# A gated attention and mixture-of-experts layer: the experts' scatter adds its rows to the residual rows already stored in the output

## The chip, the cores and the metric

The kernel runs on one core of one Trainium2 chip. The metric is the device time of one execution in microseconds (us); lower is better. The kernel before takes 298.14 us, the median of 3 runs (295.5 to 301.95).

## The reference, cut to what matters

There are 32 batches of 128 tokens with 128 features, so T = 4096 tokens, and 8 experts with room for 512 tokens each. A token that comes too late for its expert's room keeps its residual row unchanged.

```python
x = x + tanh(g_xattn[0]) * xattn(layernorm(x), ctx, ctx)    # 16 heads of 8, length 128
x = x + tanh(g_ffn[0])   * moe(layernorm(x))

def moe(tokens):                       # E = 8 experts, C = T / E = 512 places each
    gates = softmax(tokens @ Wg); idx = argmax(gates)
    loc = cumsum(one_hot(idx)) - 1     # the token's place with its expert; kept if loc < C
    hidden = relu(expert_in @ W1 + b1) # 128 -> 512
    expert_out = hidden @ W2 + b2      # 512 -> 128
    return gate * expert_out[idx, loc] # 0 for tokens that were not kept
```

## The kernel before, in words

The program is written by hand for each engine; semaphores are waited for in the order in which the code stands. It has two stages.

**Attention.** A loop over steps c from -8 to 39 runs a software pipeline over the 32 batches, in groups of four (GB = 4, eight groups). At step c the scores of batch c are computed on TensorE (PE, tile S, L482), and VectorE (DVE) takes their row maxima (L833, negm). One step later the maxima are transposed, split by ScalarE (ACT, L720) and DVE (L839) into two bf16 rows (tile mrow, 16 x 2 x 128), and SyncE (SP) sends them with two DMAs of 4 KB (L358) into the free rows of qp, the packed queries. After they have landed, PE computes the shifted scores of that batch (tile TS, L497, two steps after the batch began), ACT their exponentials (prob, L703), and PE the values (O, L513). For each group SP also packs the queries and keys of a coming group with 12 DMAs of 128 KB (L347, pack), loads x and the context (L377 and L372), and stores the finished residual rows x1 of an old group to the output (L368). All of these are on SP's one DMA queue.

Each group of tokens ends in a tile rec (three buffers, used in turn). A row of rec holds, in order, the normalised row (128 numbers), the residual row x1 (128) and 8 logits; the first logit's place is later overwritten by the gate, the second's by a code of the token's number. The first REC = 258 numbers of it are the token's record. GpSimd (POOL) scatters the records into rec_dram in device memory with indirect DMAs of 128 rows (scatter, L1224), at the place that the routing has found: expert times 512 plus place with that expert. Places that no token takes must read as zero, so POOL clears all of rec_dram beforehand with eight DMAs from a tile of zeros (zero_records, L1272), one in each of the steps c = 1 to 8. The scatter of the first group waits for them.

**Experts.** When all records have landed, SP loads for each expert e the normalised rows (load_xe, tile xe, 512 B a row) and, with a second DMA, the rest (load_xr, tile xr: residual row, gate, code; 520 B a row). PE transposes xe (turn, L608), computes the hidden layer (hidden, L618) and the outputs (outputs, L634); the order on PE is turn(e), outputs(e-2), hidden(e), so that the outputs of an expert come two turns after its rows (experts 5 and 6 then follow one another). DVE does half of the ReLUs (relus, L1110) and closes each expert: residual2(e) reads gate and code from xr, takes tanh(g_ffn) into the gate, turns the code into a token number (tok), and starts fin as b2 times gate plus the residual row (L1125, 4 instructions); finish(e, h) adds gate times the expert's output to half h of fin (L1140). POOL writes fin to the output with four indirect DMAs for each expert (rows_out, L1313), 128 rows of 512 B each. The tile fin has two buffers, so residual2(e) first waits until the four scatters of expert e-2 have landed (semaphore fin_out). The order on DVE is relus(e), finish(e-1, 0), residual2(e), finish(e-1, 1), and PE may write half h of the output banks again (X) after finish of the expert before (v_fin). After the last scatter SP waits for all of them and the program ends.

Of the kernel before, what the change touches and what calls it, by code (L numbers as in the profile page):

```python
# [32 lines left out]
REC = 2 * P + 2  # L33
# [3 lines left out]
def flamingo_kernel(nc, x, ctx_in, g_xattn, g_ffn, w_qkv, b_qkv, w_out, b_out, wg, w1, b1, w2, b2, consts, out):  # L37
# [4 lines left out]
    DE = D + E  # L42
    HEADS = 16
# [15 lines left out]
    with ExitStack() as ctx:  # L59
# [102 lines left out]
        xe = [sb(f"xe{i}", [P, ET, D]) for i in range(2)]  # L162
        xr = [sb(f"xr{i}", [P, ET, REC - D]) for i in range(2)]
# [3 lines left out]
        gate2 = [sb(f"gate2_{i}", [P, ET]) for i in range(2)]  # L167
        tok = [sb(f"tok{i}", [P, ET], U32) for i in range(2)]
# [34 lines left out]
        w1_in, w2_in, xe_in, xr_in, fin_out = sem2("w1_in"), sem2("w2_in"), sem2("xe_in"), sem2("xr_in"), sem2("fin_out")  # L203
# [90 lines left out]
        def _(sp):  # L294
# [54 lines left out]
            def step(c):  # L349
# [15 lines left out]
                if stores:  # L365
                    sp.wait_ge(v_x1, GB * (g - 2) + GB)
                    sl = bass.ds((g - 2) * GB, GB)
                    sp.dma_start(out_v[:, sl, :], rec[(g - 2) % 3][:, :, D:2 * D]).then_inc(x1_out[(g - 2) % 3], 16)  # L368
# [31 lines left out]
            for e in range(2):  # L400
                load_xr(e)
            sp.wait_ge(p_eT, 1)
            load_xe(2)

            for e in range(2, E):
                sp.wait_ge(p_H, 4 * (e - 1))
                load_w1(e)
                if e < E - 1:
                    sp.wait_ge(p_eT, e)
                    load_xe(e + 1)  # L410
                sp.wait_ge(p_Y, 2 * (e - 1))
                load_w2(e)
                sp.wait_ge(v_res, e - 1)
                load_xr(e)
# [7 lines left out]
        def _(pe):  # L422
# [179 lines left out]
            def turn(e):  # L602
# [4 lines left out]
                for t in range(ET):  # L607
                    mm = nc.tensor.transpose(S[:, e % 2, t * P:(t + 1) * P], xe[e % 2][:, t, 0:D], ident)  # L608
# [50 lines left out]
        def _(act):  # L659
# [45 lines left out]
            def step(c):  # L705
# [65 lines left out]
                if j == 1 and is_group(g - 2) and g - 2 < NG - 1:  # L771
# [3 lines left out]
                    nc.scalar.activation(rec[G % 3][:, :, 2 * D + 1], token_code[:, G * GB:(G + 1) * GB], ACT.Copy)  # L775
# [5 lines left out]
            def normed2(ks):  # L781
                for k in ks:
                    nc.scalar.activation(rec[(NG - 1) % 3][:, k, 0:D], rec[(NG - 1) % 3][:, k, D:2 * D], ACT.Identity,
# [6 lines left out]
            nc.scalar.activation(rec[(NG - 1) % 3][:, :, 2 * D + 1], token_code[:, (NG - 1) * GB:], ACT.Copy).then_inc(a_code, 1)  # L790
# [28 lines left out]
        def _(dve):  # L819
# [38 lines left out]
            def residual(n):  # L858
                dve.wait_ge(p_at, n + 1)
                dve.wait_ge(g_xb, n // GB + 1)  # L860
                G, row1 = n // GB, rec[n // GB % 3][:, n % GB, D:D + DE]
# [45 lines left out]
            def route(G):  # L907
# [4 lines left out]
                lgs = rec[G % 3][:, :, 2 * D:2 * D + E]  # L912
# [438 lines left out]
```

## Time and profile before

| What | us |
|---|---|
| median of 3 runs | 298.14 |
| the profiled execution, its own time | 298.6 |
| its span, first to last instruction | 296.5 |
| outside the span | 2.1 |
| attention, until the last residual row | about 207 |
| last routing, last records, first expert's rows | about 207 to 221 |
| experts on PE | 221 to 286.9 |
| last scatter's issue and landing, end | 286.8 to 296.5 |

Times in the profile are counted from the first instruction. PE is the matmul engine, PEld its weight loads, "SPq" and "POOLq" the time in which SyncE or GpSimd issue a DMA or wait in their instruction queue. PEclk is the clock that the chip granted to TensorE, as a share of 2.4 GHz. In the chain of waits each row is one piece of the chain that ended last; a row that begins with DMA is a transfer that something waited for.

### The profile page before, as it was taken

What the parts mean: (1) busy time and instruction counts of PE and PEld (TensorE: products, weight loads), DVE (VectorE), ACT (ScalarE), POOL (GpSimd) and SP (SyncE); (2) the same over time, 40 slices, a digit from 0 to 9 for tenths busy, and PEclk for the clock granted to TensorE, in tenths of its full rate; (3) what the DMA queues carried; (4) which work ended last, traced back from release to release, by engine and by line L of the source; (5) the groups of instructions that cost most, each with busy time, mean ns of one, the idle gap of its engine ahead of it and who ended that gap; (6) DMA issues with size and microseconds to landing.
All of it is one profiled execution on the core that took longest, in us unless ns stands there. A gap on an engine that the chain in (4) does not pass through costs nothing.

```text
span 296.5 us, 8184 instructions
## 1 busy us (share of the span) xinstructions
PE 244.5 (82%) x2907; PEld 163.5 (55%) x2907; DVE 196.6 (66%) x663; ACT 155.6 (52%) x375; POOL 182.3 (61%) x246
## 2 busy tenths in 40 slices
PE   1748758788979989999899989995869999999950
PEld 1325525465755755765656666663324677777740
DVE  4676717647978999989897999965302545555440
ACT  5553727567778787787887756681202322222100
POOL 6625916911982998897897968448720056555781
PEclk9998959969999999999999999999595999999995
DMA  4652771990482652661733541138352256554310
GB/s 120 184 162 73 214 217 32 237 293 19 113 235 57 174 158 71 195 182 46 213 110 90 152 126 57 58 102 174 138 144 66 71 170 188 173 180 132 103 55 16
DMA packets 50920, 39.27 MB, mean 132 GB/s; under 512 B 9698, under 2 KB 47223, under 8 KB 50880
## 3 DMA queue, kind: packets, MB, share of 16 engines
q1 hardware_dynamic: 47168, 28.67, 35.9%
q0 software_dynamic: 3712, 10.07, 10.4%
q8 instruction: 24, 0.39, 0.6%
q14 instruction: 16, 0.13, 0.2%
HBM read 13.72 MB, written 12.65 MB: 89 GB/s over the span
## 4 chain that ended last, share of the span: by engine, by line
PE 39%; DVE 13%; DMA 13%; SPq 10%; issue 9%; ACT 8%; POOL 4%; POOLq 0%; ACTq 0%; DVEq 0%
PE X L634 9%; DMA qp<-mrow 8%; DVE negm L833 6%; SPq L347 6%; PE TS L618 5%; PE M L546 3%; ACT prob L703 3%; PE O L513 3%; PE TS L497 3%; PE O L618 3%; PE M L618 2%; PE S L482 2%; PE X L441 2%; SPq L358 2%; POOL rec_dram L1224 2%
## 5 line engine op out<-in xcount | busy, mean ns | idle before, releaser
L703 ACT ACTIVATE prob<-TS 128x512 f32<-128x512 f32 x128 | 72.0, 589 | 40.1 <-PE TS L497 39.2
L833 DVE TENSOR_REDUCE negm<-S 128x4 f32<-128x512 f32 x128 | 81.6, 679 | 8.5 <-PE S L482 7.9
L513 PE MATMUL O<-prob,vals 128*32 128x128 f32 x1024 | 42.1, 283 | 0.8 <-ACT oraw L712 0.8
L1313 POOL DMA_INDIRECT out_dram<-fin,tok x32 | 31.5, 986 | 14.2 <-issue 12.2
L1224 POOL DMA_INDIRECT rec_dram<-rec,slot x32 | 32.2, 1005 | 8.0 <-issue 5.5
L497 PE MATMUL TS<-qp,kp 64*128 64x128 bf16 x512 | 28.1, 221 | 9.7 <-DMA qp<-mrow 9.6
L482 PE MATMUL S<-kp,qp 62*128 62x128 bf16 x512 | 31.3, 222 | 2.3 <-DVE negm L833 2.0
L513 PEld LDWEIGHTS O<-prob,vals 128*32 128x32 f32 x1024 | 24.6, 110 | 13.9 <-ACT prob L703 7.0
L267 POOL TENSOR_TENSOR rest_k<-full_k,parts_k 128x512 f32<-128x512 f32 x7 | 8.0, 1149 | 39.3 <-ACT parts_k L674 39.3
L804 ACT ACTIVATE qp<-TS,b_act 128x512 f32<-128x512 f32 x16 | 11.0, 687 | 39.9 <-PE TS L618 39.9
L634 PE MATMUL X<-w2s,qp 128*128 128x128 f32 x240 | 28.2, 275 | 0.9 <-issue 0.9
L634 PEld LDWEIGHTS X<-w2s,qp 128*128 128x128 f32 x240 | 27.4, 192 | 1.7 <-ACT qp L804 1.7
L482 PEld LDWEIGHTS S<-kp,qp 62*128 62x128 bf16 x512 | 18.0, 95 | 14.4 <-issue 6.3
L497 PEld LDWEIGHTS TS<-qp,kp 64*128 64x128 bf16 x512 | 19.1, 96 | 11.8 <-DMA qp<-mrow 11.3
L1168 POOL TENSOR_TENSOR fence_p<-pool_c 128x1 f32<-128x1 f32 x16 | 3.2, 201 | 27.6 <-DVE tok L1122 20.3
L618 PE MATMUL TS<-xeT,w1s 128*128 128x512 f32 x32 | 18.4, 659 | 1.4 <-ACT xeT L799 1.4
L1175 POOL TENSOR_TENSOR rs<-rs,pool_c 128x4 f32<-128x4 f32 x16 | 16.5, 1029 | 1.3
L1140 DVE SCALAR_TENSOR_TENSOR fin<-X,gate,fin 128x128 f32<-128x128 f32 x30 | 9.2, 345 | 11.8 <-PE X L634 11.8
L839 DVE TENSOR_TENSOR mrow<-M,mrow 16x128 bf16<-16x128 f32 x32 | 8.8, 275 | 11.9 <-ACT mrow L720 11.5
L546 PE MATMUL M<-cst,oraw 128*128 128x128 f32 x64 | 14.2, 304 | 2.3 <-DVE mrow L839 1.9
L683 ACT ACTIVATE xn<-x_sb,nm,rs 128x128 f32<-128x128 f32 x32 | 13.8, 481 | 3.0 <-POOL nm L1187 3.0
L538 PE MATMUL X<-wout_g,onT 128*128 128x136 f32 x64 | 13.7, 296 | 1.4 <-ACT onT L766 1.4
(170 smaller groups left out, 486.8 us busy)
## 6 DMA issues: line engine op xcount, KB each, us to landing
kp<-parts_k SPq DMA_DIRECT2D x48, 128.0 KB, 2.5
qp<-parts_q SPq DMA_DIRECT2D x48, 128.0 KB, 4.1
rec_dram<-zeros POOLq DMA_DIRECT2D x8, 516.0 KB, 6.2
xr<-rec_dram SPq DMA_DIRECT2D x8, 260.0 KB, 3.9
x_sb<-in_x_dram SPq DMA_DIRECT2D x8, 256.0 KB, 3.6
c_sb<-in_ctx_dram SPq DMA_DIRECT2D x8, 256.0 KB, 3.5
out_dram<-rec SPq DMA_DIRECT2D x8, 256.0 KB, 3.3
w1s<-in_L_ffn_W_dram SPq DMA_DIRECT2D x8, 256.0 KB, 4.1
```

The lines of the kernel that those rows point to most:

```text
L347: sp.dma_start(dst, src).then_inc((k_in if side == "k" else q_in)[H % 3], 16)
L482: mm = nc.tensor.matmul(S[:, a, i * L:(i + 1) * L], qp[b][rows, h, t0:t0 + L], kp[b][rows, h, t0:t0 + L], start=True, stop=True)
L497: mm = nc.tensor.matmul(TS[:, a, i * L:(i + 1) * L], kp[b][rows, h, t0:t0 + L], qp[b][rows, h, t0:t0 + L], start=True, stop=True)
L513: mm = nc.tensor.matmul(o_out[i * HV:(i + 1) * HV, u * L:(u + 1) * L], vals[G % 2][:, k, h, :], prob[n % 2][:, h * L:(h + 1) * L], start=( ...
L546: mm = nc.tensor.transpose(back_out[:, u * L:(u + 1) * L], oraw[(c - 4) % 2][:, u * L:(u + 1) * L], ident)
L618: nc.tensor.matmul(bank, w1s[e % 2][:, f * P:(f + 1) * P], xeT[e % 2][:], start=True, stop=True).then_inc(p_H, 1)
L634: mm = nc.tensor.matmul(out_tile(e, h, i), hid[e % 2][:, f, t * P:(t + 1) * P], w2s[e % 2][:, f, :], start=(f == 0), stop=(f == FC - 1))
L703: nc.scalar.activation(prob[n % 2][:, first:first + 4 * L], TS[:, a, :], ACT.Exp).then_inc(a_exp, 1)
L833: V.tensor_reduce(negm[n % 2][:, first:first + 4], S[:, a, :].rearrange("p (h k) -> p h k", k=L), AX.X, ALU.max, negate=True).then_inc(v_r ...
L1175: return G_.tensor_tensor(rs[:, 1, :], rs[:, 0, :], pool_c[:, 1, :], ALU.pow)
L1224: G_.indirect_dma_start(rec_dram, bass.IndirectOffsetOnAxis(slot[p][:, k:k + 1], 0), rec[p][:, k, 0:REC], None, bounds_check=T - 1, oob_is ...
L1313: G_.indirect_dma_start(out_rows, bass.IndirectOffsetOnAxis(tok[p][:, t:t + 1], 0), fin[p][:, t, :], None, bounds_check=T - 1, oob_is_err= ...
```

## The change

A record is half as long: gate, code and the normalised row, 130 numbers (520 B) in place of 258 (1032 B). For that the row of rec is laid out anew (x1 first, then the logits, whose last two places take gate and code, then the normalised row), so that the record is one contiguous piece. The residual row is no longer in it. rec_dram, the tile of zeros and the eight clearing DMAs are half as large, and the scatters of records send 520 B a row. xe holds the whole record; load_xr and the tile xr are gone. The residual reaches the output by the stores of the attention stage that were there before (L368); the expert's scatter now adds to the row stored there (compute_op=ADD). Rows of tokens that no expert kept were already right by those stores.

DVE's residual2 is in two parts. codes(e), which reads gate and code from xe, comes ahead of relus(e) and waits for xe; gate2 and tok have four buffers instead of two. bias2(e), in the place of residual2(e), starts fin as b2 times gate with one tensor_scalar for each 128 rows. The load of xe(e + 1) waits for codes(e - 1) as well, since codes reads the buffer.

```diff
-REC = 2 * P + 2
+REC = P + 2
+    GATE, CODE = DE - 2, DE - 1
-        xe = [sb(f"xe{i}", [P, ET, D]) for i in range(2)]
-        xr = [sb(f"xr{i}", [P, ET, REC - D]) for i in range(2)]
+        xe = [sb(f"xe{i}", [P, ET, REC]) for i in range(2)]
...
             def load_xe(e):
-                sp.dma_start(xe[e % 2][:], rec_v[e][:, :, 0:D]).then_inc(xe_in[e % 2], 16)
-            def load_xr(e):
-                sp.dma_start(xr[e % 2][:], rec_v[e][:, :, D:REC]).then_inc(xr_in[e % 2], 16)
+                sp.dma_start(xe[e % 2][:], rec_v[e]).then_inc(xe_in[e % 2], 16)
...
             for e in range(2):
                 load_xe(e)
-            for e in range(2):
-                load_xr(e)
             sp.wait_ge(p_eT, 1)
+            sp.wait_ge(v_tok, 1)
             load_xe(2)
             for e in range(2, E):
...
                 if e < E - 1:
                     sp.wait_ge(p_eT, e)
+                    sp.wait_ge(v_tok, e)
                     load_xe(e + 1)
                 sp.wait_ge(p_Y, 2 * (e - 1))
                 load_w2(e)
-                sp.wait_ge(v_res, e - 1)
-                load_xr(e)
...
-            def residual2(e):
-                p = e % 2
-                dve.wait_ge(xr_in[p], 16 * (e // 2) + 16)
+            def codes(e):
+                dve.wait_ge(xe_in[e % 2], 16 * (e // 2) + 16)
+                if e >= 4:
+                    dve.wait_ge(fin_out[e % 2], 64 * (e // 2 - 1))
+                V.tensor_scalar(gate2[e % 4][:], xe[e % 2][:, :, 0], tg[:, 1:2], None, ALU.mult).then_inc(v_gate2, 1)
+                V.tensor_scalar(tok[e % 4][:], xe[e % 2][:, :, 1], -1.0, float(NONE), ALU.mult, ALU.add).then_inc(v_tok, 1)
+            def bias2(e):
                 if e >= 2:
-                    dve.wait_ge(fin_out[p], 64 * (e // 2))
-                V.tensor_scalar(gate2[p][:], xr[p][:, :, D], tg[:, 1:2], None, ALU.mult).then_inc(v_gate2, 1)
-                V.tensor_scalar(tok[p][:], xr[p][:, :, D + 1], -1.0, float(NONE), ALU.mult, ALU.add).then_inc(v_tok, 1)
+                    dve.wait_ge(fin_out[e % 2], 64 * (e // 2))
                 dve.wait_ge(v_gate2, e + 1)
                 for t in range(ET):
-                    mm = V.scalar_tensor_tensor(fin[p][:, t, :], b2_all[:, e, :], gate2[p][:, t:t + 1],
-                                                xr[p][:, t, 0:D], ALU.mult, ALU.add)
+                    mm = V.tensor_scalar(fin[e % 2][:, t, :], b2_all[:, e, :], gate2[e % 4][:, t:t + 1], None, ALU.mult)
                 mm.then_inc(v_res, 1)
...
-                G_.indirect_dma_start(rec_dram, bass.IndirectOffsetOnAxis(slot[p][:, k:k + 1], 0), rec[p][:, k, 0:REC], None,
+                G_.indirect_dma_start(rec_dram, bass.IndirectOffsetOnAxis(slot[p][:, k:k + 1], 0), rec[p][:, k, GATE:DE + D], None,
                                       bounds_check=T - 1, oob_is_err=False).then_inc(sent[p], 16)
...
-                    G_.indirect_dma_start(out_rows, bass.IndirectOffsetOnAxis(tok[p][:, t:t + 1], 0), fin[p][:, t, :], None,
-                                          bounds_check=T - 1, oob_is_err=False).then_inc(fin_out[p], 16)
+                    G_.indirect_dma_start(out_rows, bass.IndirectOffsetOnAxis(tok[e % 4][:, t:t + 1], 0), fin[p][:, t, :], None,
+                                          bounds_check=T - 1, oob_is_err=False, compute_op=ALU.add).then_inc(fin_out[p], 16)
```

On DVE, in the middle of the expert stage of the kernel before, one expert is ReLUs (qp), the first half of finish (fin<-X), then gate, tok and the four starts of fin, then the second half of finish:

```order
400 L1113 COPY b_dve<-b_all 128x4
401 L1110 TENSOR_SCALAR qp<-O,b_dve 128x512
402 L1110 TENSOR_SCALAR qp<-M,b_dve 128x512
403 L1140 SCALAR_TENSOR_TENSOR fin<-X,gate_1,fin 128x128 x2
404 L1121 TENSOR_SCALAR gate_0<-xr,tg 128x4
405 L1122 TENSOR_SCALAR tok<-xr 128x4
406 L1125 SCALAR_TENSOR_TENSOR fin<-b_all,gate_0,xr 128x128 x4
407 L1140 SCALAR_TENSOR_TENSOR fin<-X,gate_1,fin 128x128 x2
```

The same place on DVE in the changed kernel:

```order
401 L1114 TENSOR_SCALAR gate_2<-xe,tg 128x4
402 L1115 TENSOR_SCALAR tok<-xe 128x4
403 L1107 COPY b_dve<-b_all 128x4
404 L1104 TENSOR_SCALAR qp<-O,b_dve 128x512
405 L1104 TENSOR_SCALAR qp<-M,b_dve 128x512
406 L1137 SCALAR_TENSOR_TENSOR fin<-X,gate_1,fin 128x128 x2
407 L1123 TENSOR_SCALAR fin<-b_all,gate_2 128x128 x4
408 L1137 SCALAR_TENSOR_TENSOR fin<-X,gate_1,fin 128x128 x2
```

Gate and tok have moved ahead of the ReLUs of their expert, and only the four starts of fin stand between the two halves of finish.

On SP's DMA queue, at the start of the expert stage of the kernel before (the first store is that of the last residual rows):

```order
91 L368 DMA out_dram<-rec 128x4x128
92 L390 DMA xe<-rec_dram 128x4x128 x2
93 L394 DMA xr<-rec_dram 128x4x130 x2
94 L390 DMA xe<-rec_dram 128x4x128
95 L310 DMA w1s<-in_L_ffn_W_dram 128x512
96 L390 DMA xe<-rec_dram 128x4x128
97 L313 DMA w2s<-in_L_ffn_W_dram 128x4x128
98 L394 DMA xr<-rec_dram 128x4x130
```

The same place in the changed kernel:

```order
91 L368 DMA out_dram<-rec 128x4x128
92 L390 DMA xe<-rec_dram 128x4x130 x3
93 L310 DMA w1s<-in_L_ffn_W_dram 128x512
94 L390 DMA xe<-rec_dram 128x4x130
95 L313 DMA w2s<-in_L_ffn_W_dram 128x4x128
96 L310 DMA w1s<-in_L_ffn_W_dram 128x512
```

The two loads of xr behind the first loads of xe are gone, and so is the one behind each w2s. On POOL the order is the same; eight DMAs from the zeros and 32 record scatters are narrower there (130 numbers in place of 258). PE and ACT run the same instructions in the same order.

## Rows read from the trace of the kernel before

**Rows 1.** The page's granted clock in 40 slices of 7.4 us, in tenths.

```profile
PEclk9998959969999999999999999999595999999995
```

**Rows 2.** Chain of waits, attention: start us, us, what.

```profile
35.73 4.56 DMA qp<-mrow
...
53.57 5.12 DMA qp<-mrow
...
60.81 6.19 DMA qp<-mrow
...
122.93 2.42 DMA qp<-mrow
```

**Rows 3.** Clearing DMAs: line L1272's durations, first and last start, and timeline.

```profile
L1272 POOL DMA_DIRECT2D rec_dram<-zeros x8: 721/778/937, 31.0 to 82.0; - x8
...
52.95 1.50 POOL L1272 DMA_DIRECT2D rec_dram<-zeros  x2 [0.49 <-issue]
57.90 0.72 POOL L1272 DMA_DIRECT2D rec_dram<-zeros  x1
59.87 0.81 POOL L1272 DMA_DIRECT2D rec_dram<-zeros  x1
```

**Rows 4.** Table by stage: stretch, length, busy PE, PEld, DVE, ACT, POOL, PEclk, DMA share, GB/s.

```profile
52.00:59.00 7.00, 4.79 (x81) 3.47 (x78) 5.12 (x12) 4.20 (x12) 6.32 (x9) 0.92 0.95 238
59.00:66.00 7.00, 6.83 (x78) 4.61 (x72) 2.76 (x9) 4.61 (x11) 1.68 (x2) 0.60 1.06 298
```

**Rows 5.** Timeline of ACT, the mrow copy of steps 5, 9, 13 and 17.

```profile
52.70 0.25 ACT L720 ACTIVATE mrow<-M 16x128 bf16<-16x128 f32 x1
...
78.46 0.25 ACT L720 ACTIVATE mrow<-M 16x128 bf16<-16x128 f32 x1
...
100.20 0.25 ACT L720 ACTIVATE mrow<-M 16x128 bf16<-16x128 f32 x1
...
121.06 0.25 ACT L720 ACTIVATE mrow<-M 16x128 bf16<-16x128 f32 x1
```

**Rows 6.** Chain of waits between the last records and the first expert.

```profile
215.82 2.30 DMA rec_dram<-rec,slot
218.17 2.77 DMA xe<-rec_dram
```

**Rows 7.** Timeline of expert 2 to 3: DVE's wait for the scatters, POOL's scatters.

```profile
246.20 0.23 DVE L1121 TENSOR_SCALAR gate<-xr,tg 128x4 f32<-128x4 f32 x1 [1.98 <-DMA out_dram<-fin,tok]
...
250.21 0.97 POOL L1313 DMA_INDIRECT out_dram<-fin,tok  x1 [0.30 <-issue]
...
252.51 0.23 DVE L1121 TENSOR_SCALAR gate<-xr,tg 128x4 f32<-128x4 f32 x1 [0.85 <-DMA out_dram<-fin,tok]
```

**Rows 8.** Chain of waits, outputs of experts 2 and 3.

```profile
249.23 3.57 PE X L634 x32
...
256.68 3.57 PE X L634 x32
```

**Rows 9.** Timeline of POOL: the first scatter of expert 5 and the last of all.

```profile
274.81 1.11 POOL L1313 DMA_INDIRECT out_dram<-fin,tok  x1 [0.53 <-issue]
...
289.33 0.97 POOL L1313 DMA_INDIRECT out_dram<-fin,tok  x1 [0.30 <-issue]
```

**Rows 10.** Groups by line and shape: count, busy us, mean ns, idle before.

```profile
L1224 POOL DMA_INDIRECT rec_dram<-rec,slot x32 | 32.2, 1005 | 8.0 <-issue 5.5 <-DVE rec L865 1.2 <-ACT rec L783 0.5
L1313 POOL DMA_INDIRECT out_dram<-fin,tok x32 | 31.5, 986 | 14.2 <-issue 12.2 <-DVE fin L1140 2.1
...
L1125 DVE SCALAR_TENSOR_TENSOR fin<-b_all,gate,xr 128x128 f32<-128x128 f32 x32 | 9.2, 347 | 0.0
...
L1082 DVE TENSOR_SCALAR wout_g<-wout,tg 128x128 f32<-128x128 f32 x1 | 0.3, 274 | 0.0
```

**Rows 11.** The page's DMA issues: KB each, median us to landing.

```profile
rec_dram<-zeros POOLq DMA_DIRECT2D x8, 516.0 KB, 6.2
...
out_dram<-fin,tok POOLq DMA_INDIRECT x32, 3.0
```

More of the change, by code:

```diff
@@ L166, in flamingo_kernel @@
                for i in range(2)]
-        gate2 = [sb(f"gate2_{i}", [P, ET]) for i in range(2)]
-        tok = [sb(f"tok{i}", [P, ET], U32) for i in range(2)]
+        gate2 = [sb(f"gate2_{i}", [P, ET]) for i in range(4)]
+        tok = [sb(f"tok{i}", [P, ET], U32) for i in range(4)]
         fin = [sb(f"fin{i}", [P, ET, D]) for i in range(2)]
@@ L789, in _ @@
             nc.scalar.activation(lexp[:], ldif[:], ACT.Exp).then_inc(a_lexp2, 1)
-            nc.scalar.activation(rec[(NG - 1) % 3][:, :, 2 * D + 1], token_code[:, (NG - 1) * GB:], ACT.Copy).then_inc(a_code, 1)
+            nc.scalar.activation(rec[(NG - 1) % 3][:, :, CODE], token_code[:, (NG - 1) * GB:], ACT.Copy).then_inc(a_code, 1)
             normed2(range(1, GB))
@@ L964, in route2 @@
             def route2(G):
-                lgs = rec[G % 3][:, :, 2 * D:2 * D + E]
+                lgs = rec[G % 3][:, :, D:DE]
                 spread = [P, GB, E]
@@ L1139, in finish @@
                             mm.then_inc(v_fin, 1)
-                    mm = V.scalar_tensor_tensor(fin[p][:, t, :], out_tile(e, h, i), gate2[p][:, t:t + 1],
+                    mm = V.scalar_tensor_tensor(fin[p][:, t, :], out_tile(e, h, i), gate2[e % 4][:, t:t + 1],
                                                 fin[p][:, t, :], ALU.mult, ALU.add)
@@ L1146, in _ @@
             dve.wait_ge(v_b1, 1)
+            codes(0)
             relus(0)
-            residual2(0)
+            bias2(0)
             for e in range(1, E - 1):
+                codes(e)
                 relus(e)
                 finish(e - 1, 0)
-                residual2(e)
+                bias2(e)
                 finish(e - 1, 1)
@@ L1155, in _ @@
             finish(E - 2, 1)
+            codes(E - 1)
             relus(E - 1)
-            residual2(E - 1)
+            bias2(E - 1)
             finish(E - 1, 0)
@@ L1203, in norm2 @@
             def norm2(G):
-                to, spread = rec[G % 3][:, :, 0:D], [P, GB, D]
+                to, spread = rec[G % 3][:, :, DE:DE + D], [P, GB, D]
                 if G >= 1:
@@ L1209, in norm2 @@
                 scaled(G)
-                G_.tensor_tensor(to, rec[G % 3][:, :, D:2 * D], mv2[:, :, 0:1].broadcast_to(spread), ALU.subtract).then_inc(g_sub2, 1)
+                G_.tensor_tensor(to, rec[G % 3][:, :, 0:D], mv2[:, :, 0:1].broadcast_to(spread), ALU.subtract).then_inc(g_sub2, 1)
                 pool.wait_ge(g_rs2, G + 1)
```

20 lines of the change are left out of this document (10 added, 10 removed).

## The prediction, on record before the changed kernel ran

> **What bounds the kernel now.** I read the chain of waits first, then the stages' table, then the timeline of the expert stage and its end, because the change touches three places: the clearing DMAs in the attention stage, the passage from the last records to the first expert, and the experts' scatters.
>
> In the attention stage the chain runs through PE, DVE and ACT, but at three points it hangs on one 4 KB transfer, the two DMAs that bring the shifts into qp (mrow). It lasts 4.56, 5.12 and 6.19 us there, and 2.42 us at a later point of the chain [rows 2]. The three slow ones lie between 35 and 67 us. The clearing of rec_dram runs from 31.0 to 82.0, eight DMAs of 516 KB that land in 6.2 us (median) [rows 3, 11]. In the stretches 52 to 59 and 59 to 66 us the 16 DMA engines are busy 0.95 and 1.06 of the time, at 238 and 298 GB/s, while DVE works 5.12 and 2.76 of 7 us [rows 4]: the small transfer waits behind others, and the engines wait for it. Later pack transfers and loads are as many, without that effect, so I put the excess down to the clearing. The pace agrees: the mrow copy of step 5 is at 52.70, of step 9 at 78.46, of step 13 at 100.20 and of step 17 at 121.06 [rows 5], so four batches take 25.8, 21.7 and 20.9 us. The clock granted to TensorE is at its lower level (1.2 GHz) for most of slice 6 (37.1 to 44.5 us), and for much of slice 9 (59.3 to 66.7) [rows 1, 4], each time after PE had stood waiting for mrow.
>
> Between the stages the chain goes through the last record scatters (2.30 us for the last one) and the load of expert 0's rows (2.77 us) [rows 6]. Then PE works without a gap: outputs of two successive experts begin at 249.23 and 256.68, a period of 7.45 us [rows 8]. From expert 5 on POOL is the later one: its 12 last scatters begin at 274.81 and the last begins at 289.33, 14.52 us for 11 steps, 1.32 each with the fences; the span ends at 296.5, 7.2 us later [rows 9].
>
> **The change, part by part** (minus is a gain; all against the profiled execution).
>
> *Clearing, half the bytes.* In 52 to 66 us the engines moved 14 us x 268 GB/s (mean) = 3.75 MB [rows 4]. Four clearing DMAs start there (two from 52.95 on, and those at 57.90 and 59.87), 2.11 MB [rows 3, 11]. Halving them takes away 1.06 MB, 3.9 us of saturated transfer. The two chain pieces are (5.12 - 2.4) + (6.19 - 2.4) = 6.5 us above the undisturbed 2.4, and these four batches took 25.8 - 20.9 = 4.9 us more than the later ones [rows 2, 5]. Bounds: 0 (pack transfers alone would hold mrow up) and -4.9. I take half the excess of the chain pieces, -3.3. For the piece of 4.56 us at 35.7 the excess is 2.2 us; three clearing DMAs start from 31.0 on. Bounds 0 and -2.2; as all three are shortened I take -1.4. The eighth clearing DMA (82.0) and the record scatters, now 520 B a row, lie in steps that are 21.7 against 20.9 us: bounds 0 and -0.9, taken -0.4. Together -5.1. The lower clock behind the first two stalls is part of those 25.8 us and is not counted again. If the clearing were slower by packets than by bytes, this term would shrink: I see no row for a clearing of 520 B rows, hence the bound of 0.
>
> By the Trainium skill (DMA: Bandwidth & Descriptors, "Issuing engines are not separate DMA queues") DMAs issued by SyncE and by GpSimd run on the same 16 engines and interleave, which is what would let a GpSimd clearing delay a SyncE shift. The trace agrees: 4.56 to 6.19 us for mrow beside clearing DMAs, 2.42 without.
>
> *Records and first rows.* The last record scatter carries half the bytes, and behind the first two loads of xe there is no xr load any more. The two pieces of the chain are 2.30 and 2.77 us [rows 6]; a plain scatter of 512 B rows still takes 3.0 us to land (median) [rows 11], so latency is most of it. Bounds 0 and -1.0, taken -0.5. POOL's own time for a scatter doesn't follow the bytes: 1005 ns for 1032 B rows, 986 for 512 B [rows 10]. SP has eight DMAs fewer to issue, but nothing waits for SP there: 0. Load xe(e + 1) now waits for codes(e - 1) too; DVE reaches that right behind finish(e - 3, 1), about when the turn that it waited for before is done, and PE needs the rows a period (7.45) later: 0, and up to 0.5 once if late.
>
> *DVE in the expert stage.* codes moves 2 small instructions ahead of the ReLUs; the start of fin goes from 347 ns to that of a tensor_scalar of the same shape, 274 [rows 10]. PE sets the pace, so no gain: 0. What stands behind bias2(e) in DVE's order is finish(e - 1, 1), and PE's second half of outputs(e) waits for that.
>
> *The scatter that adds.* The trace has no adding DMA, so there are three unknowns.
> First, POOL's time for one. Nearest rows: 1005 and 986 ns for plain ones [rows 10]. Below: nothing gained. Above: twice as much, if POOL has to describe a read of the old row beside each write. I take +0.10. In the tail it counts for 12 scatters: +1.2.
> Second, landing. Plain: 3.0 median, and the end comes 7.2 us after the last begins [rows 9, 11]. An add reads the output row before it writes it. Bounds 0 and +2.8 (one more load like the 2.77 of xe [rows 6]); I take +0.7, since the reads of a DMA's rows overlap. Counted once, at the end.
> Third, the ring that this closes: scatters of expert e - 2 land, bias2(e), finish(e - 1, 1), scatters of e - 1, landing. DVE's two waits for it ended at 246.20 and 252.51 [rows 7], so the ring took 6.3 us, 1.1 less than PE's period; gate and tok (0.4 us) leave it and the starts of fin lose 0.3, which makes the room about 1.8. In the ring my +0.7 and 2 x 0.1 fit. PE is safe by more, at first: finish(1, 1) ends before 246.20 + 2 x 0.23 + 4 x 0.35 + 2 x 0.35 = 248.8, and the second half of outputs(2) begins at 249.23 + 1.8 = 251.0. Cost 0.
>
> By the Trainium skill (Collectives: The Full Stack, "The bandwidth ceiling: the fold count and why AG ≠ RS ≠ AR") a reducing transfer has two source reads and emits two read descriptors for each chunk where a copy emits one. No run here shows it yet. By it POOL would write three descriptors a row where it wrote two; if its whole 0.99 us went by descriptors, that would be an estimated +0.5 a scatter and +6 us in the tail, so the sum would come out near no change.
>
> *Sum*: -5.1 - 0.5 + 1.2 + 0.7 = -3.7. 298.6 - 3.7 = 294.9; the profiled execution is 0.5 above the median of 298.14, so 294.4.
>
> **The rivals.**
> A, *the stalls go altogether.* With half the bytes the queue drains between clearing DMAs, mrow lands in 2.4 us, PE no longer waits long enough to lose its clock, and all of 4.9 + 2.2 + 0.9 = 8.0 us comes back. For it: the DMA share at the saturated stretches is only just 1, and waiting grows fast near there. Against: SP's pack DMAs still come in bursts. With -0.5 and +0.5 for the adding: 298.1 - 8.0 = 290.1.
> B, *clearing was not the cause.* The 12 pack transfers and the loads of x and context in the same steps hold the shift up. Against it: they are as many in later groups, where mrow took 2.42 us. Or the bytes are halved and the packets' time is not. Then only -0.5 and +1.9 are left: 299.5.
> C, *slower: POOL's price for an adding scatter.* Place: the 32 scatters. Price x each. In the tail it costs 12x. A plain one takes POOL 0.97 us and 0.30 before it, 1.27 [rows 7]. While four scatters fit into 7.45 us, PE still sets the pace: 4 (1.27 + x) + 0.35 for the fence = 7.45 gives x = 0.5. Beyond, five periods stretch by 4 (x - 0.5) each. It takes back all of the gain at x = 0.4 (12 x 0.4 = 4.8, and 0.7 for landing), and from x = 0.65 the kernel is over 6 us slower. With x = 0.99, double: 12 + 5 x 2.0 + 0.7 - 5.6 = +17, 315. The same comes about if the DMA engines do the rows' adds one after another and a landing takes over 1.8 us more: the ring then passes PE's period. For it: nothing in this trace excludes it. Against: a plain scatter's time hardly depends on what it carries.
>
> **How the numbers follow.** A measurement of this kernel can tell about 2%, 6 us: the three runs spread over 6.5. Forecast 0.50, A 0.24, B 0.11, C 0.15. Predicted 294.4. Own range of the forecast 291 to 297.5. The range goes down to 289.0, beyond A, and up to 303.0, which leaves out the worse part of C and a little below A. Faster by over 2% (below 292.2): 0.8 of A and 0.2 of the forecast, 0.29, and a little for both together at once, so 0.30. Slower by over 2% (above 304.1): most of C, 0.14. Within: 0.56.
>
> **What would show it right or wrong.** Clearing: the chain's mrow pieces between 35 and 67 us at 3 to 4 us, and the mrow copies of steps 5 and 9 about 22.5 us apart; 21 is A, 25 or more is B. The clearing DMAs land in about 4 us instead of 6.2. Passage: last record scatter to the first turn 4.6 instead of 5.1 us. Adding: a scatter on POOL at 1.1 us; 12 of them in 16 us; above 1.4 us C begins. The end 8 us behind the last scatter's start. PE without a gap between its experts, at 7.45 us; a gap before outputs would say that the ring has become the bound, and the forecast is then wrong even if the clearing gave all it could.

## The result, and the profile of the changed kernel

The changed kernel takes 301.08 us, the median of 11 runs (299.08 to 308.65). The kernel before, run beside it again, takes 298.07 (11 runs, 295.5 to 304.66). The ratio is 1.0115, 95% interval 1.0065 to 1.0165. The change costs about 3 us here where I forecast a gain of 3.7; the time lies inside my range and within 2%, but on the other side of no change. Ratios and their intervals leave out executions in a slower state of the chip, while medians and ranges are of all runs.

The page of the changed kernel, profiled once: its span, the granted clock in 40 slices, then three groups (count, busy us, mean ns of one, idle before them and what ended most of it).

```profile
span 299.2 us, 8186 instructions
...
PEclk9989987999999999999999999986879999999885
...
L1313 POOL DMA_INDIRECT out_dram<-fin,tok x32 | 49.8, 1556 | 12.9 <-issue 11.4
...
L1224 POOL DMA_INDIRECT rec_dram<-rec,slot x32 | 32.1, 1002 | 8.1 <-issue 5.5
...
L1123 DVE TENSOR_SCALAR fin<-b_all,gate 128x128 f32<-128x128 f32 x32 | 7.5, 311 | 21.8 <-DMA out_dram<-fin,tok 21.8
...
rec_dram<-zeros POOLq DMA_DIRECT2D x8, 260.0 KB, 4.3
...
out_dram<-fin,tok POOLq DMA_INDIRECT x32, 3.3
```

Read against [rows 10, 11], one number stands out. An adding scatter holds POOL for 1556 ns where a plain one took 986. The record scatters, with half the bytes, still hold it for 1002 (1005 before). The clearing DMAs land in 4.3 us instead of 6.2, the expert scatters in 3.3 instead of 3.0 (medians). And DVE now stands 21.8 us waiting for scatters to land.

The attention stage did what the change was to do for it. In the chain of waits (start, us, what) the shift's transfers answer to [rows 2], and the last two rows below to [rows 6].

```profile
34.55 2.34 DMA qp<-mrow
...
50.88 4.55 DMA qp<-mrow
...
57.33 3.31 DMA qp<-mrow
...
116.11 2.17 DMA qp<-mrow
...
208.51 2.19 DMA rec_dram<-rec,slot
...
210.75 2.92 DMA xe<-rec_dram
```

Two of the three slow transfers shrank by 2.2 and 2.9 us and the third by 0.6. In the stages' table the two stretches of [rows 4] now read as follows (busy us of PE, PEld, DVE, ACT, POOL; granted clock; DMA share; GB/s).

```profile
52.00:59.00 7.00, 5.45 (x95) 3.86 (x94) 5.05 (x15) 4.94 (x14) 4.86 (x5) 1.00 0.86 215
59.00:66.00 7.00, 6.70 (x103) 3.81 (x103) 5.34 (x15) 5.28 (x12) 0.00 (x0) 1.00 0.30 83
```

In the second stretch the DMA engines are busy 0.30 of the time and not 1.06, and DVE works 5.34 us of 7 in it, not 2.76. The clock that the chip granted to TensorE changed with it: 1.00 in that stretch where it was 0.60, and 0.8 and 0.9 in slices 6 and 9 of the page, where [rows 1] has 0.5 and 0.6 (slice 7 now has 0.7). What part of the gain came through the clock was not separated. ACT's copies of mrow in steps 5, 9, 13 and 17, to be read against [rows 5], show where the time was won.

```profile
50.02 0.25 ACT L714 ACTIVATE mrow<-M 16x128 bf16<-16x128 f32 x1
...
72.11 0.25 ACT L714 ACTIVATE mrow<-M 16x128 bf16<-16x128 f32 x1
...
93.54 0.25 ACT L714 ACTIVATE mrow<-M 16x128 bf16<-16x128 f32 x1
...
114.14 0.25 ACT L714 ACTIVATE mrow<-M 16x128 bf16<-16x128 f32 x1
```

Step 5 is 2.68 us earlier than before, step 9 6.35, step 13 6.66, step 17 6.92. From step 5 to step 9 it is 22.1 us (25.8 before). The record scatter's landing and the first load of xe take 2.19 + 2.92 us, no less than the 2.30 + 2.77 of before. So expert 0's rows are transposed at 213.71, 7.3 us earlier than 220.99.

Then POOL. Its timeline (start, us, what, idle before) gives the first scatter of the expert stage, three in the tail, and the last; it answers to [rows 9].

```profile
232.66 1.59 POOL L1313 DMA_INDIRECT out_dram<-fin,tok  x1 [2.61 <-issue]
...
264.22 1.56 POOL L1313 DMA_INDIRECT out_dram<-fin,tok  x1 [0.16 <-issue]
...
272.09 1.56 POOL L1313 DMA_INDIRECT out_dram<-fin,tok  x1 [0.16 <-issue]
...
279.61 1.56 POOL L1313 DMA_INDIRECT out_dram<-fin,tok  x1 [0.16 <-POOL fence_p L1168]
...
292.74 1.55 POOL L1313 DMA_INDIRECT out_dram<-fin,tok  x1 [0.30 <-issue]
```

The whole difference is in these two ends. The first scatter starts 7.35 us earlier than before (240.01). From first to last it is 60.08 us where it was 49.32, 10.76 more. From the last one's start to the end of the span it is 6.46 us instead of 7.17, 0.7 less. Together: -7.35 + 10.76 - 0.7 = +2.7, the difference of the spans (299.2 - 296.5). The question left is what the 10.76 us consist of. The waits of the expert stage, 213 to 299 us, name two candidates (who waits for whom: us in all, count, us of the longest).

```profile
DVE fin L1123 <- DMA out_dram<-fin,tok: 21.8, 5, 5.7
...
PE X L628 <- DVE fin L1137: 3.4, 4, 2.5
POOL out_dram L1313 <- DVE fin L1137: 1.3, 1, 1.3
```

One is POOL's own time (32 times 0.57 us more). The other is the ring of landing, bias2, finish and scatter, which makes DVE wait 21.8 us and PE 3.4.

### The profile page after: what moved, and what is told of

Read it like the earlier page. It is cut to its first block, busy times and chain, and to the rows that moved or that the text cites. A ratio compares the mean times of both kernels' runs of the same rounds, so it can differ in the third digit from the quotient of the medians.

```text
span 299.2 us, 8186 instructions
## 1 busy us (share of the span) xinstructions
PE 244.4 (82%) x2907; PEld 163.2 (55%) x2907; DVE 193.1 (65%) x663; ACT 155.6 (52%) x375; POOL 200.6 (67%) x246
## 3 DMA queue, kind: packets, MB, share of 16 engines
HBM read 11.62 MB, written 8.45 MB: 67 GB/s over the span
## 4 chain that ended last, share of the span: by engine, by line
PE 28%; issue 16%; DVE 14%; DMA 13%; POOL 11%; ACT 9%; SPq 7%; POOLq 1%; ACTq 0%; DVEq 0%
DVE negm L827 6%; POOL out_dram L1313 6%; DMA qp<-mrow 5%; SPq L347 4%; PE O L507 3%; PE M L540 3%; DMA c_sb<-in_ctx_dram 3%; ACT prob L697 3%; PE S L476 3%; PE TS L612 3%; PE TS L491 3%; DMA out_dram<-fin,tok 2%; PE X L435 2%; POOL rec_dram L1224 2%; PE X L628 2%
## 5 line engine op out<-in xcount | busy, mean ns | idle before, releaser
L1313 POOL DMA_INDIRECT out_dram<-fin,tok x32 | 49.8, 1556 | 12.9 <-issue 11.4
L1224 POOL DMA_INDIRECT rec_dram<-rec,slot x32 | 32.1, 1002 | 8.1 <-issue 5.5
L628 PE MATMUL X<-w2s,qp 128*128 128x128 f32 x240 | 30.3, 282 | 4.5 <-DVE fin L1137 3.4
L628 PEld LDWEIGHTS X<-w2s,qp 128*128 128x128 f32 x240 | 28.5, 195 | 6.3 <-DVE fin L1137 4.2
L1168 POOL TENSOR_TENSOR fence_p<-pool_c 128x1 f32<-128x1 f32 x16 | 7.3, 457 | 21.8 <-DVE fin L1137 20.3
L1123 DVE TENSOR_SCALAR fin<-b_all,gate 128x128 f32<-128x128 f32 x32 | 7.5, 311 | 21.8 <-DMA out_dram<-fin,tok 21.8
L612 PE MATMUL TS<-xeT,w1s 128*128 128x512 f32 x32 | 19.3, 689 | 1.4 <-ACT xeT L793 1.4
L760 ACT ACTIVATE onT<-M 128x128 f32<-128x128 f32 x32 | 8.9, 278 | 10.8 <-PE M L556 10.7
```

The costliest lines, as they stand in the source:

```text
L612: nc.tensor.matmul(bank, w1s[e % 2][:, f * P:(f + 1) * P], xeT[e % 2][:], start=True, stop=True).then_inc(p_H, 1)
L628: mm = nc.tensor.matmul(out_tile(e, h, i), hid[e % 2][:, f, t * P:(t + 1) * P], w2s[e % 2][:, f, :], start=(f == 0), stop=(f == FC - 1))
L1224: G_.indirect_dma_start(rec_dram, bass.IndirectOffsetOnAxis(slot[p][:, k:k + 1], 0), rec[p][:, k, GATE:DE + D], None, bounds_check=T - 1, ...
L1313: G_.indirect_dma_start(out_rows, bass.IndirectOffsetOnAxis(tok[e % 4][:, t:t + 1], 0), fin[p][:, t, :], None, bounds_check=T - 1, oob_is_ ...
```

## The experiments

I called the theories P (POOL's price for each adding scatter sets the expert stage), R (the ring of landings sets it), and K (the halved clearing is what gains in attention). The expectations call K "theory C", its opposite, that the clearing has no part in it, "theory S", and use N for a cost of the changed order on DVE. Chips differ: the kernel before takes 298.5 us on one of those used here and 309.6 to 310.7 on the other three. So a kernel is compared by its ratio to the kernel before on its own chip, and by places in its trace.

**The scatter without the add.** The changed kernel, one argument removed:

```diff
-                                          bounds_check=T - 1, oob_is_err=False, compute_op=ALU.add).then_inc(fin_out[p], 16)
+                                          bounds_check=T - 1, oob_is_err=False).then_inc(fin_out[p], 16)
```

> The changed kernel with the experts' scatter as a plain write again (the residual is missing from the rows that an expert kept; nothing else is left out). Theory P (POOL's own time for an adding scatter, 1.55 us in place of 0.97, is the whole loss behind the attention stage): the scatter is back at 0.97 to 1.0 us and a slot at 1.27, the first of them starts at about 232.7, the last 12 are again packed behind PE's outputs of experts 5 and 6, the last starts near 282.0 and the whole takes 290 to 291.5 us, 2.3 to 2.8% less than the kernel before. Theory R (landing: the ring from the scatter's landing over bias2 and finish back to the scatter): the same total, but the landing falls by over 1 us. Theory N (the changed order on DVE, codes ahead of the ReLUs, costs part of it): over 293 us and a gap on PE that remains.

Measured: 301.5 us beside 309.59 for the kernel before, ratio 0.9749 (0.969 to 0.9808). The profiled execution was its longest, 307.75. Its group of scatters:

```profile
L1313 POOL DMA_INDIRECT out_dram<-fin,tok x32 | 31.3, 977 | 17.4 <-issue 10.5
```

The first to the last scatter take 51.25 us (247.35 to 298.60), and the end follows 7.2 us after the last one starts. Without the add the rest of the change is a gain of 2.5%. With it, the changed kernel stands at 1.0115, 1.0193 and 1.0006 times the kernel before in its three comparisons. So the add costs between 2.6 and 4.6% of the time; the two kernels were never run side by side. P and R expected the same total here, so this run shows that the add is the cause and not which way it works. What POOL's part can be is seen from 977 against 1556 ns.

The count of DMA packets on GpSimd's queue shows what changes with the add (packets, MB, share of 16 engines): first without it, then the changed kernel.

```profile
q0 software_dynamic: 2688, 6.04, 6.4%
...
q0 software_dynamic: 6272, 6.04, 12.3%
```

The bytes are the same and the packets 3584 more, 112 for each scatter of 128 rows (and as many more in the next experiment), and the queue's share of the DMA engines' time is nearly double.

**The add alone, in the kernel before.**

```diff
-                                          bounds_check=T - 1, oob_is_err=False).then_inc(fin_out[p], 16)
+                                          bounds_check=T - 1, oob_is_err=False, compute_op=ALU.add).then_inc(fin_out[p], 16)
```

> The kernel before with only the experts' scatter turned into an adding one (rows that an expert kept hold the residual twice). Records, clearing, the order on DVE and the two buffers of tok stay as before. Theory P: a scatter takes POOL 1.55 us, its last one starts about 10 us later than at 289.3, and the whole takes 307 to 310 us. Theory N: under 304, since the order on DVE is the old one. If the adding's price came from the record's shape, the scatter would stay under 1.2 us here.

Measured: 324.05, ratio 1.0452 (1.037 to 1.0534). Its chain through the expert stage goes from landing to landing:

```profile
252.35 6.11 DMA out_dram<-fin,tok
...
263.10 5.87 DMA out_dram<-fin,tok
...
273.63 5.48 DMA out_dram<-fin,tok
...
283.77 5.12 DMA out_dram<-fin,tok
...
293.55 3.50 DMA out_dram<-fin,tok
```

and its waits (us in all, count, us of the longest):

```profile
DVE gate L1121 <- DMA out_dram<-fin,tok: 31.1, 5, 7.8
...
PE X L634 <- DVE fin L1140: 11.1, 5, 4.1
```

POOL's price is the same (the page has 1558 ns) but the stage is longer: 70.1 us from first to last scatter, and the chain's landings stand 10.75, 10.5, 10.1 and 9.8 us apart. In this kernel the chain says R (four buffers for fin were not tried in it). DVE waits for the landing before gate, tok and the four starts of fin, and PE waits 11.1 us for DVE. The changed kernel has those off the ring (codes comes earlier, the starts of fin are cheaper, nothing of xr is read), and its stage is 10 us shorter with the same scatters. That part of the change, which I had costed at nothing, is worth these 10 us once the scatter adds; its parts were not tried one by one.

**Four buffers for fin.** In the changed kernel a landing is then waited for only four experts later:

```diff
-        fin = [sb(f"fin{i}", [P, ET, D]) for i in range(2)]
+        fin = [sb(f"fin{i}", [P, ET, D]) for i in range(4)]
...
             def bias2(e):
-                if e >= 2:
-                    dve.wait_ge(fin_out[e % 2], 64 * (e // 2))
```

> The changed kernel with four buffers for fin instead of two, and one semaphore for each, so that bias2(e) waits for nothing but what codes(e) has waited for. Theory P: DVE's 21.8 us of waiting for landings and PE's gaps go, but POOL, whose 32 slots of 1.86 us are nearly back to back, gains only its own gaps of some 2 us: 0 to 1% below the changed kernel. Theory R (the ring is the bound): 1.5 to 3% below it, and POOL's slots shrink or it is idle between experts.

The changed kernel itself ran beside it:

> The changed kernel itself, unaltered, for a comparison on the same chip as the other runs of this group: 1.0 to 1.6% over the kernel before, a scatter at 1.55 us on POOL. If the chip of the first group comes again, where the kernel before took 309.6 us, about 313. By theory C the kernel with the full clearing would then be some 5 us above it, by theory S within 1.5 us.

Measured: 302.23, ratio 1.0195 (1.0064 to 1.0326), beside 302.91, ratio 1.0193 (1.004 to 1.0346), for the changed kernel. But its five runs fall apart: 302.23, 302.83 and 303.5, on which that ratio rests, and 297.22 (the profiled one) and 300.59, both below all four of the changed kernel (301.36 to 304.52). The four-buffer kernel's group of scatters, as the grouping by lines has it:

```profile
L1312 POOL DMA_INDIRECT out_dram<-fin,tok x32 | 49.8, 1556 | 11.0 <-issue 9.8 <-POOL fence_p L1167 1.0 <-DVE fin L1136 0.3
```

and its first two and its last scatter on POOL:

```profile
230.67 1.59 POOL L1312 DMA_INDIRECT out_dram<-fin,tok  x1 [2.60 <-issue]
232.56 1.58 POOL L1312 DMA_INDIRECT out_dram<-fin,tok  x1 [0.30 <-issue]
...
288.94 1.55 POOL L1312 DMA_INDIRECT out_dram<-fin,tok  x1 [0.30 <-issue]
```

DVE's waits for landings are gone from its trace, all 21.8 us of them, and PE's for DVE too. Yet POOL still takes 58.27 us from first to last, 31 x 1.88: one scatter behind the other, with nothing but 0.3 us of issue and the fences between. The changed kernel took 60.08, 61.11 and 60.79 in its three profiles. So by the traces R is worth 1.8 to 2.8 us of the span, and P is the bound. The times can't confirm that size: by the medians it is 0.7 us, by the two low runs some 4, and the intervals reach 4 us and more to either side. (Of the 6.1 us by which the profile at 297.22 is shorter than the changed kernel's beside it, 3.3 lie ahead of the first scatter, which four buffers don't touch.) A wait of 21.8 us on DVE cost about a tenth of itself, since POOL would have been busy all the same.

**Half a row added.** The same number of rows with half the bytes, run once.

```diff
-                    G_.indirect_dma_start(out_rows, bass.IndirectOffsetOnAxis(tok[e % 4][:, t:t + 1], 0), fin[p][:, t, :], None,
+                    G_.indirect_dma_start(out_rows, bass.IndirectOffsetOnAxis(tok[e % 4][:, t:t + 1], 0), fin[p][:, t, 0:D // 2], None,
```

> The changed kernel with only the first 64 columns of a row in the adding scatter (the other half of the kept tokens' rows stays at the residual). If POOL's 0.58 us more for an adding scatter is the price of more descriptors a row, it stays at 1.5 to 1.6 us and the whole within 1 us of the changed kernel; if it goes by bytes, the scatter is at 1.2 to 1.3 us and the whole falls by some 6 us.

```profile
L1313 POOL DMA_INDIRECT out_dram<-fin,tok x32 | 49.9, 1559 | 11.9 <-issue 10.6 <-DVE fin L1137 1.2 <-POOL fence_p L1168 0.2
```

1559 ns for 256 B a row, as for 512, and the packets of the queue are again 6272. POOL's price goes by whether the rows are added, and not by bytes. That it goes by rows fits with the packets, but every scatter here has 128 rows, so that is not shown. The time was 298.94 in this one run, and first to last scatter 59.1 us; a single run can't tell that time from the changed kernel's.

**The clearing made full again.** The changed kernel with a second DMA of 256 KB behind each clearing DMA, into a tensor that nothing reads:

```diff
+                pool.dma_start(pad_dram[i * (T // ZEROED):(i + 1) * (T // ZEROED), :].rearrange("(p a) c -> p a c", p=P),
+                               zeros[:, 0:P].unsqueeze(1).broadcast_to([P, T // P // ZEROED, P])).then_inc(s_padded, 16)
```

> The changed kernel with the clearing doubled again: behind each clearing DMA of 260 KB comes one of 256 KB into a tensor that nobody reads, so the bytes cleared are those of the kernel before, and records stay short. Theory C (the clearing's bytes delay the shifts, mrow): the three mrow pieces of the chain return to 4 to 6 us, the steps 5 to 9 take 25 to 26 us instead of 22.1, the first expert scatter starts 5 to 7 us later, and the whole takes 305 to 308. Theory S (the gain in the attention stage came from the shorter record scatters or by chance of the clock): within 1.5 us of the changed kernel, 300 to 302.5.

The first time the changed kernel was not beside it: 313.92 against 309.59 for the kernel before, ratio 1.0144 (1.0085 to 1.0203). So both ran once more on one chip.

> The changed kernel once more, unaltered, as the partner on one chip of the next three. 1.0 to 1.9% over the kernel before.

> The changed kernel with the clearing's bytes doubled again, as before in the first group, now beside the changed kernel on the same chip. In the traces so far the mrow copy of step 24 stands at 156.9 to 158.3 us in three executions with the full clearing and at 149.1 to 155.3 in six with the short one. Theory C: 1.5 to 2.5% over the changed kernel, and step 24 at 156 to 159. Theory S: under 0.7% over it.

Measured: the changed kernel 310.58, ratio 1.0006 (0.9965 to 1.0047); with the full clearing 314.17, ratio 1.0108 (1.0048 to 1.0168). One over the other is 1.0102, some 3 us: more than theory S allowed (0.7%) and less than theory C asked for (1.5%). In the chain of the padded kernel the shift's transfers are slow again:

```profile
35.92 3.65 DMA qp<-mrow
...
53.67 5.60 DMA qp<-mrow
...
61.16 4.38 DMA qp<-mrow
...
85.19 4.58 DMA qp<-mrow
```

where the changed kernel on the same chip has

```profile
34.95 2.36 DMA qp<-mrow
50.45 3.78 DMA qp<-mrow
56.13 4.02 DMA qp<-mrow
```

and ACT's copy of mrow in step 24 comes at 159.08 instead of 152.76. This is so in every kernel whose clearing goes over all eight steps: with the full clearing that copy is at 158.30 (before), 156.90, 157.93 and 159.08; with the short one at 151.04 (the changed kernel), 155.27, 153.62, 149.12, 149.84, 152.62, 152.76 and 151.86. The means are 158.05 and 152.0, 6.0 us apart, and the two sets don't overlap. (157.93 and 155.27 are from the longest execution of their kernel; without these two the means are 6.5 apart.) The granted clock alone doesn't explain it: from 31 to 45 us it was 0.50 and 0.64 in the padded kernel and 0.99 and 0.77 in the changed one beside it, but the changed kernel whose copy is at 153.62 had 0.50 and 0.57 there. K holds, at 6 us.

Why then only 3 us in the time? Expert 0's rows are loaded 6.7 us later (227.31 against 220.65), the first scatter only 2.45 later. The kernels' POOL timelines show where most of that goes. With the full clearing:

```profile
243.34 0.31 POOL L1171 TENSOR_TENSOR fence_p<-pool_c 128x1 f32<-128x1 f32 x1 [17.31 <-DVE fin L1140]
244.11 1.59 POOL L1318 DMA_INDIRECT out_dram<-fin,tok  x1 [0.46 <-issue]
```

The changed kernel on the same chip:

```profile
238.46 0.31 POOL L1168 TENSOR_TENSOR fence_p<-pool_c 128x1 f32<-128x1 f32 x1 [19.08 <-DVE fin L1137]
241.66 1.59 POOL L1313 DMA_INDIRECT out_dram<-fin,tok  x1 [2.88 <-issue]
```

Between the fence and the first scatter POOL stands idle for 2.88 us in one and 0.46 in the other, and neither waits for an engine. The padded kernel has a few more instructions on POOL ahead of that place, and I see no other difference there. The fence itself is 4.9 us later, not 6.7: the padded kernel gained 1.8 us ahead of it, where PE ran expert 0's first matmuls at a granted clock of 1.00 (226 to 240 us) and the changed one at 0.79 (226 to 233). So of the 6.7 us, less 1.8 and 2.4, some 2.5 are left at the first scatter; the stage is 0.8 us longer (61.62 against 60.79) and the end 0.6, which makes the 3.9 us between the two spans (312.8 and 308.9). Where POOL sets the pace of the whole stage, the 2.4 us should count in full; that is argued, not tried. What the idle time is I have not found out.

**Clearing at quieter times.** If the clearing is what delays the shift, it might go where no shift is due. In the kernel before, four pairs of clearing DMAs in steps 3, 4, 7 and 8, each behind the shifted scores of a batch:

```diff
-                for i in ((c - 1,) if 0 <= c - 1 < ZEROED else ()):
-                    zero_records(i)
+                quiet = {3: 0, 4: 2, 7: 4, 8: 6}
+                if c in quiet:
+                    pool.wait_ge(p_T, 4 * (c - 2) + 1)
+                    for i in range(2):
+                        zero_records(quiet[c] + i)
```

> The kernel before with nothing changed but the time at which POOL clears: the eight DMAs of 516 KB go out two by two in steps 3, 4, 7 and 8, when SP packs nothing, each pair behind the shifted scores of the batch two steps back. Theory C (the bytes hurt because they meet the packing and mrow): the chain's mrow pieces fall to 2.4 to 3.5 us, step 24 comes at 151 to 154 instead of 158.3, and the whole takes 1 to 2% less than the kernel before. Theory S: no change within 0.7%. If POOL's new waits delay its splits, it is slower.

A miss: 314.35 beside 310.39 for the kernel before, ratio 1.0066 (1.0015 to 1.0117), slower and not faster. Its chain:

```profile
39.56 5.97 DMA qp<-mrow
...
54.32 5.00 DMA qp<-mrow
...
65.94 5.79 DMA qp<-mrow
...
87.72 3.68 DMA qp<-mrow
```

The pairs started at 38.48, 51.01, 64.78 and 82.03 on POOL, and the slow transfers of the chain start 1 to 6 us behind them. The copy in step 24 is at 161.12, later than with any other clearing. POOL now waits ahead of two pairs (2.65 and 7.43 us), but its splits of keys behind them still wait for ACT (3.69 and 3.43 us), so I see no sign that these waits made it slower. A pair moves 1 MB, and a shift is due every five to six us, so I see no place here where it passes between two of them.

**A rebuilt residual.** If the short records gain 6 us and the add costs 9, one wants the first without the second. This kernel writes into the record the row's mean (negative) and standard deviation, 132 numbers in all. DVE rebuilds the residual row from the normalised one, ahead of the ring; the scatter is plain.

```diff
-REC = P + 2
+REC = P + 4
...
+                for t in range(ET):
+                    mm = V.tensor_scalar(res[e % 4][:, t, :], xe[e % 2][:, t, 4:REC], xe[e % 2][:, t, 1:2],
+                                         xe[e % 2][:, t, 0:1], ALU.mult, ALU.subtract)
...
-                                          bounds_check=T - 1, oob_is_err=False, compute_op=ALU.add).then_inc(fin_out[p], 16)
+                                          bounds_check=T - 1, oob_is_err=False).then_inc(fin_out[p], 16)
```

> A version meant to keep the gain and leave out the price: records of 132 numbers (mean with its sign turned, standard deviation, gate, code, normalised row), clearing and loads nearly as short as in the changed kernel; the residual row is rebuilt on DVE as normalised row times deviation plus mean, into a tile of its own, and the experts' scatter is a plain write again. Only finish waits for the landings. Costs: 4 more DVE instructions an expert (about 1.2 us of a 7.45 us period), two small POOL instructions a group. Theory P with C: 2.3 to 3.3% below the kernel before, like the plain scatter of the first group. If the two POOL instructions delay the attention stage, 1 to 2%.

> The version with the rebuilt residual once more, in five rounds, since its first comparison was wide (0.954 to 1.001). Theory P with C: 1.6 to 3% below the kernel before, with an interval wholly below 1; its plain scatter at 0.97 us, PE without a gap among the experts.

Measured: 292.31, ratio 0.9776 (0.9542 to 1.001), and on another chip 303.18, ratio 0.9856 (0.9763 to 0.9949). The two groups that matter in the first:

```profile
L1325 POOL DMA_INDIRECT out_dram<-fin,tok x32 | 31.9, 995 | 10.6 <-issue 9.7 <-DVE res L1120 0.6 <-DVE fin L1146 0.3
...
L1120 DVE TENSOR_SCALAR res<-xe 128x128 f32<-128x128 f32 x32 | 9.3, 355 | 0.0
```

POOL is back at 995 ns, and the 32 new instructions of 355 ns on DVE lie in time that DVE spent waiting. The last scatter starts at 283.27, 6.1 us before that of the kernel before, and the span is 6.1 us shorter (290.4). The first scatter is 8.2 us earlier (it too has the short idle time before it, 0.52 us, and not 2.66); but with plain scatters PE sets the pace of the first experts, so that head start is not carried to the end. This version beats both kernels: the kernel before by 1.4 to 2.2%, of which the second comparison is clear of noise (and a little under the 1.6 to 3% expected), and the changed kernel on the first chip by 3.5% (292.31 against 302.91, no run of one among those of the other).

**Both together**: the rebuilt residual with the pairs of the experiment before it.

> The version with the rebuilt residual and short records, plain scatter, and the clearing in the quiet steps as well. Theory C: its short clearing costs 1 to 3 us still, which go: 2.5 to 3.5% below the kernel before, step 24 at 149 to 152. Theory S: like the rebuilt version, 2.2% below.

Measured: 304.62, ratio 0.9837 (0.9778 to 0.9895), against 0.9776 and 0.9856 without the pairs: no gain from them that the intervals show, and short of the 2.5 to 3.5% that theory C expected.

## Why the prediction was wrong

*Clearing, -5.1.* The mechanism was right and the term a little small: -6.0 by the means of step 24, -7.3 in the changed kernel's own profile. The chain pieces fell from 4.56, 5.12 and 6.19 to 2.34, 4.55 and 3.31 us, where I had written 3 to 4, and steps 5 and 9 are 22.1 us apart for my 22.5. It lies between my forecast and rival A (-8.0). Rival B, that the clearing was not the cause, has fallen: filling the bytes up again brings the slow transfers back. By the Trainium skill (DMA: Bandwidth & Descriptors, "Issuing engines are not separate DMA queues") the transfers of both engines' queues interleave on the same 16 engines; the padded kernel agrees, since bytes issued by GpSimd alone, read by nobody, lengthen SyncE's 4 KB shift from 2.36, 3.78 and 4.02 us to 3.65, 5.60 and 4.38 on one chip.

*Records and first rows, -0.5.* It was 0: 5.07 us before, 5.11 now. Half the bytes made neither transfer shorter, as the bound of 0 had it.

*DVE in the expert stage, 0.* Right against PE's pace, and yet an important part. Had the add come without it, the ring would have cost what the second experiment shows.

*POOL's time for an adding scatter, +0.10 each, +1.2 in all.* This is the step that failed. Measured: +0.57 each (1556 against 986 ns). I had both ends, 0 and +0.99, and chose near the lower one because the trace showed 1005 ns for 1032 B and 986 for 512 B, as if the price hardly depended on what a scatter carries. It doesn't depend on the bytes, and the half-row kernel shows that again at 1559 ns. But an add is not more bytes, and rows of the trace that differ in bytes alone can say nothing on it. By the Trainium skill (Collectives: The Full Stack, "The bandwidth ceiling: the fold count and why AG ≠ RS ≠ AR") a reducing transfer has two source reads, so two read descriptors for each chunk; the trace agrees in size, +0.57 us for my estimate of +0.5 by that rule, and the half-row kernel in that bytes don't matter. It shows 112 more packets a scatter, but no reads: the page counts 11.62 MB read from device memory with and without the add. That estimate stood in the prediction, with a sum near no change, and I didn't use it.

The count was too small as well. At 12 scatters in the tail, +0.57 would be 6.8 us. But an expert's four scatters now take POOL 4 x 58.27 / 31 = 7.52 us with the gaps, just over PE's 7.45, so POOL is the later one in the whole stage and not from expert 5 on. The four-buffer kernel, where only POOL counts, took 58.27 - 49.32 = 9.0 us more than plain scatters.

*Landing, +0.7.* The median rose by 0.3 (3.0 to 3.3), and the end came 0.7 us sooner behind the last scatter's start instead of 0.7 later.

*The ring, 0.* It was 1.8 to 2.8 us. I had put 0.1 for each of two scatters into its room of 1.8 us. With 0.57 each, and POOL so full that all four stand one behind the other, the ring is 2.3 us longer. So this error follows from the first.

*Rival C* was the mechanism. I gave it 0.15. Its own formula with the measured x = 0.57 gives 12 x 0.57 + 5 x 4 x 0.07 = 8.2, so 298.1 - 5.6 + 8.2 + 0.7 = 301.4, for 301.08 measured. That it comes so close is partly luck: measured were -7.35 for its -5.6, +10.8 (POOL and the ring) for its +8.2, and -0.7 for its +0.7. Its period is wrong too: 4 (1.27 + 0.57) + 0.35 = 7.71 us, where POOL took 7.52, since in the trace an expert's fence starts while the scatter ahead of it still runs. I had said in it that all of the gain is gone from x = 0.4. What went wrong was thus one price, between ends that I knew, taken near the wrong one. In the sum with measured sizes: -7.35 to the first scatter, +9.0 for POOL, +1.8 for the ring, -0.7 at the end, +2.7.

## What to carry to other kernels

An indirect DMA that adds costs its issuing engine more, here 1.56 us for a scatter of 128 rows against 0.98, and bytes saved don't pay for it; count it on the issuing engine, for all such scatters, and see whether that engine then becomes the pace. When a row of the trace shows that a price doesn't follow one quantity, that says nothing about another: take the middle of the range for an operation the trace doesn't have. Where a value can be rebuilt by an engine that waits anyway (here 32 x 355 ns on DVE), that may be cheaper than either carrying it or having the DMA add it.

## What the runs showed that I had not expected

- An adding scatter of 128 rows held POOL for 1556 to 1559 ns, with rows of 512 B or of 256 B; a plain one for 977 to 1007 ns, with rows of 512, 520 or 1032 B.
- The end came 6.4 to 6.5 us after the start of the last adding scatter (changed kernel, add in the kernel before, four buffers, half row), though that scatter takes POOL 0.57 us longer, and 7.1 to 7.2 us after the start of a plain one (before, without the add, rebuilt). In the padded kernel, which adds and has one more wait at its end, it was 7.1. Why is open.
- POOL's idle time between the fence and the first expert scatter is 2.6 to 2.9 us in most kernels, plain or adding, and 0.46 to 0.52 in those whose program on POOL is a little longer ahead of it. This was not tried by itself.
- In the chains, the shift's 4 KB transfer takes 1.6 to 2.8 us after the clearing, 3.7 to 6.0 behind a pair of clearing DMAs of 516 KB each, 2.4 to 6.2 with one of 516 KB in each step (2.4 at one place, 4.6 and more at the others), and 2.1 to 5.2 with one of 260 KB.
- On the chips where the kernel before takes 310 us, a wait of 5.3 to 5.7 us, ahead of a copy of onT on ACT (L760 of the changed kernel), ends between 205 and 214 us in all eight traces, and in none of those taken where it takes 298. The profile can't name what ended it. In the chain of the changed kernel there:

```profile
199.70 5.64 another core or an unknown queue
```

It is in kernels with and without the add, so it moves no ratio that I rest on, but its cause is open.
